# Reordering the entry of a blocked attention loop: the first score blocks ahead of most of the work on the character side

## What is computed

```python
# char = layernorm(x) [256, 512], ctx [25088, 512]
Q_char = char @ Wq_c.T + bq_c;  K_sub = ctx @ Wk_s.T + bk_s;  V_sub = ctx @ Wv_s.T + bv_s
char2sub = softmax(Q_char @ K_sub.T / sqrt(512)) @ V_sub
Q_sub = ctx @ Wq_s.T + bq_s;  K_char = char @ Wk_c.T + bk_c;  V_char = char @ Wv_c.T + bv_c
sub2char = softmax(Q_sub @ K_char.T / sqrt(512)) @ V_char      # 25088 rows
sub2char = interp_linear(sub2char, 256)                        # needs only 512 of those rows
gate = sigmoid(concat(char2sub, sub2char) @ Wg.T + bg)
x = x + gate * char2sub + (1 - gate) * sub2char
x = x + half_causal_attention(layernorm(x))                    # 16 heads of 64
x = x + mixture_of_experts(layernorm(x))                       # 32 routed experts and a shared one
```

## Time and profile before

| what | value |
|---|---|
| median of 3 runs | 1209.76 us (1207.69 to 1210.89) |
| span of the profiled execution, first to last instruction | 1206.7 us |
| TensorE matmul busy | 1061.1 us (88%) |
| TensorE weight load busy | 728.2 us (60%) |
| VectorE busy | 601.5 us (50%) |
| ScalarE busy | 387.8 us (32%) |
| chain that ended last, by engine | PE 71%, DMA 25%, DVE 2%, ACT 1% |
| moved by DMA | 381.44 MB, mean 316 GB/s |

### The profile page before, as it was taken

How to read it: one execution, slowest core, us unless ns; L and a number is a source line. 1 busy time by engine, 2 the same in 40 slices (tenths; PEclk the granted TensorE clock), 3 DMA queues, 4 the chain that set the end, 5 groups by cost and what they waited for, 6 DMA issues and landing times.

```text
span 1206.7 us, 16020 instructions
## 1 busy us (share of the span) xinstructions
PE 1061.1 (88%) x6374; PEld 728.2 (60%) x6374; DVE 601.5 (50%) x894; ACT 387.8 (32%) x594; POOL 3.5 (0%) x20
## 2 busy tenths in 40 slices
PE   8989999999999999999999999999876665656566
PEld 7767888878888888888766657664422222222223
DVE  2368878878878888788643365221211111111111
ACT  1245556556455465465422162100100000000000
POOL 1000000000000000000000000000000000000000
PEclk9999999999999999999999999999998989889899
DMA  9167899887787787788838305999999999999996
GB/s 351 62 209 281 311 344 333 302 311 270 270 309 272 269 309 270 272 293 278 282 129 356 134 7 228 428 426 425 363 426 426 430 429 427 426 430 427 428 427 275
DMA packets 89824, 381.44 MB, mean 316 GB/s; under 512 B 5569, under 2 KB 5697, under 8 KB 72769
## 3 DMA queue, kind: packets, MB, share of 16 engines
q1 hardware_dynamic: 89792, 381.00, 81.4%
HBM read 355.29 MB, written 25.69 MB: 316 GB/s over the span
## 4 chain that ended last, share of the span: by engine, by line
PE 71%; DMA 25%; DVE 2%; ACT 1%; issue 0%; SPq 0%; DVEq 0%
DMA wd<-in_r_down 24%; PE ps L579 7%; PE ps L578 7%; PE ps L577 7%; PE ps L591 7%; PE ps L592 7%; PE ps L590 7%; PE ps L957 3%; PE ps L880 3%; PE ps L550 2%; PE ps L563 2%; PE ps L932 2%; PE ps L967 2%; PE ps L938 2%; PE ps L901 1%; PE ps L914 1%
## 5 line engine op out<-in xcount | busy, mean ns | idle before, releaser
L577 PE MATMUL ps<-ctt_hi,q_hi 128*128 128x512 f32 x392 | 155.8, 397 | 4.4 <-ACT ctt_hi L1007 4.4
L579 PE MATMUL ps<-ctt_hi,q_lo 128*128 128x512 f32 x392 | 155.7, 397 | 0.0
L578 PE MATMUL ps<-ctt_lo,q_hi 128*128 128x512 f32 x392 | 155.7, 397 | 0.0
L591 PE MATMUL ps<-nat_lo,pt_hi 128*128 128x512 f32 x368 | 146.2, 397 | 0.0
L592 PE MATMUL ps<-nat_hi,pt_lo 128*128 128x512 f32 x368 | 145.0, 394 | 0.0
L590 PE MATMUL ps<-nat_hi,pt_hi 128*128 128x512 f32 x368 | 143.3, 389 | 0.4 <-DVE pt_lo L1251 0.3
L1559 DVE TENSOR_TENSOR hh<-sg,ps 128x256 f32<-128x256 f32 x32 | 13.5, 422 | 249.8 <-PE ps L938 249.8
L957 PE MATMUL ps<-wd,hh_t 128*32 128x512 f32 x512 | 78.9, 743 | 62.6 <-DMA wd<-in_r_down 57.4
L1011 ACT ACTIVATE nat_hi<-nat 128x2048 fp32r<-128x2048 f32 x48 | 92.0, 1917 | 82.9 <-DMA nat<-in_ctx_rows 82.9
L1241 DVE TENSOR_TENSOR ctt_lo<-ctt,ctt_hi 128x2048 fp32r<-128x2048 f32 x49 | 110.7, 2289 | 9.7 <-ACT ctt_hi L1007 9.7
L1246 DVE TENSOR_TENSOR nat_lo<-nat,nat_hi 128x2048 fp32r<-128x2048 f32 x48 | 109.9, 2289 | 6.1 <-ACT nat_hi L1011 4.3
(11 more groups left out here) (273 smaller groups left out, 1280.9 us busy)
## 6 DMA issues: line engine op xcount, KB each, us to landing
wu<-in_r_up SPq DMA_DIRECT2D x32, 2048.0 KB, 41.1
wd<-in_r_down SPq DMA_DIRECT2D x32, 2048.0 KB, 40.3
wg<-in_r_gate SPq DMA_DIRECT2D x31, 2048.0 KB, 39.2
ctt<-in_ctx_t SPq DMA_DIRECT2D x49, 1024.0 KB, 7.9
nat<-in_ctx_rows SPq DMA_DIRECT2D x48, 1024.0 KB, 7.3
strips<-turned SPq DMA_DIRECT2D x96, 256.0 KB, 5.5
pt<-strips SPq DMA_DIRECT2D x24, 1024.0 KB, 4.8
w_gate<-in_w_g_t SPq DMA_DIRECT2D x2, 1024.0 KB, 12.4
```

The source lines that it names most:

```text
L577: mm(o, qh, ctt_hi[par][:, c, :], start=(c == 0), stop=False)
L578: mm(o, qh, ctt_lo[par][:, c, :], start=False, stop=False)
L579: last = mm(o, ql, ctt_hi[par][:, c, :], start=False, stop=(c == HC - 1))
L591: mm(o, p_hi[:, w, :], n_lo[:, t, :], start=False, stop=False)
```

## The change

Nothing is computed differently; instructions and transfers change places, and buffers move so that they may.

- TensorE: `cb` goes to bank 5 and `bias2` to bank 4; then come `scores(0)`, the `w_qs` product (now in banks 6 and 7), `scores(1)`, the `sel_t` product, `vc`, `scores(2)`, the transposes of `pavg` with 12 dummy matmuls instead of 14, `s2c`, `scores(3)`, the transposes of `s2c`, and the products of the first pair.
- ScalarE: `ctt_hi` of blocks 0 and 1 moves ahead of `kc_t`; the splits of `nat` and `ctt`, the exps of the first pair and `pt_hi` of the first pair move ahead of the copies for `pavg_t` and `s2c`.
- VectorE: `q_lo` no longer waits for `cb`; the first pair's maxima, bias and turns move ahead of the work on `sc2`; the second pair is written out.
- SP: `ctt` of blocks 0 and 1 is loaded right behind `w_qs`, `nat` of blocks 0 and 1 next, and `w_vc`, `rows` and `w_gate2` behind them. The load of `nat[1]` waits for nothing any more.
- SBUF: `c_t`, `bias2` and `bqs_rep` lie where `s2c` and `s2c_t` will be; `sc2`, `pavg`, `pavg_t`, `kq_t` and `vc` where `w_qc` and `w_ks` were; `xn` where `pt` will be.

```diff
@@ buffers @@
-        xn = at("xn", [P, QT, D], F32, o)
-        c_t = at("c_t", [P, HC, NQ], F32, o + 4096)
+        xn = at("xn", [P, QT, D], F32, RINGB + 10 * kb)
+        c_t = at("c_t", [P, HC, NQ], F32, shared_low + 20480)
+        bias2 = at("bias2", [P, NQ], F32, shared_low + 24576)
+        bqs_rep = at("bqs_rep", [P, HC, P], F32, shared_low + 25600)
...
+        o = RINGB + 12 * kb
+        sc2 = at("sc2", [P, 4, NQ], F32, o)
+        pavg = at("pavg", [P, QT, NQ], F32, o + 4096)
+        pavg_t = at("pavg_t", [P, QT, NQ], F32, o + 6144)
+        o = RINGB + 13 * kb
         kq_t = at("kq_t", [P, HC, NQ], F32, o)
         vc = at("vc", [P, QT, D], F32, o + 4096)
@@ SP @@
-            sp.dma_start(rows[:, :], a["bias_rows"].partition_broadcast(P)).then_inc(s["rows_loaded"], 16)
...
-            sp.dma_start(flat(w_vc), runs(a["w_vc_t"])).then_inc(s["wvc_loaded"], 16)
-            sp.dma_start(sel_t[:, :, :], chunks(a["sel_t"])).then_inc(s["sel_loaded"], 16)
             load_columns(0, 0)
             load_columns(1, 1)
+            sp.dma_start(sel_t[:, :, :], chunks(a["sel_t"])).then_inc(s["sel_loaded"], 16)
+            load_rows(0, nat[0], nat_loaded[0])
+            load_rows(1, nat[1], nat_loaded[1])
+            sp.dma_start(flat(w_vc), runs(a["w_vc_t"])).then_inc(s["wvc_loaded"], 16)
+            sp.dma_start(rows[:, :], a["bias_rows"].partition_broadcast(P)).then_inc(s["rows_loaded"], 16)
             sp.dma_start(w_gate2[:, :, :], chunks(a["w_g_t"][D:2 * D, :])).then_inc(s["wg2_loaded"], 16)
-            load_rows(0, nat[0], nat_loaded[0])
...
             spread(0)
-            sp.wait_ge(s["s2c_in_psum"], 1)
-            load_rows(1, nat[1], nat_loaded[1])
@@ TensorE @@
-            pe.wait_ge(s["kc_ready"], 1)
-            pe.wait_ge(s["wqs_loaded"], 16)
-            weight_stationary(by_chunk(2), w_qs, kc_t, HC, s["kq_in_psum"])
             pe.wait_ge(s["rep_ready"], 1)
             for c in range(HC):
-                last = mm(ps[:, 1, 0:NQ], bqs_rep[:, c, :], kc_t[:, c, :], start=(c == 0), stop=(c == HC - 1))
+                last = mm(ps[:, 4, 0:NQ], bqs_rep[:, c, :], kc_t[:, c, :], start=(c == 0), stop=(c == HC - 1))
...
+            pe.wait_ge(s["qlo_ready"], 1)
+            scores(0, 0, banks_taken=False)
+
+            pe.wait_ge(s["wqs_loaded"], 16)
+            weight_stationary(by_chunk(6), w_qs, kc_t, HC, s["kq_in_psum"])
+
+            scores(1, 1, banks_taken=False)
...
-            keep_warm(14, 5)
+            keep_warm(12, 5)
```

More of the change, by code:

```diff
@@ L657, in _ @@
             last.then_inc(s["sc2_in_psum"], 1)
-            scores(0, 0, banks_taken=False)
-            scores(1, 1, banks_taken=False)
+            pe.wait_ge(s["bias2_ready"], 1)
+            pe.wait_ge(s["cb_ready"], 1)
+            pe.wait_ge(s["wvc_loaded"], 16)
+            for t in range(QT):
+                for c in range(HC):
+                    last = mm(ps[:, 4 + t, :], c_t[:, c, t * P:(t + 1) * P], w_vc[:, c, :], start=(c == 0), stop=(c == HC - 1))
+            last.then_inc(s["vc_in_psum"], 1)
+            scores(2, 0)
+            pe.wait_ge(s["vc_ready"], 1)
             pe.wait_ge(s["pavg_ready"], 1)
-            pe.wait_ge(s["vc_ready"], 1)
             transposes(pavg, ps[:, 4, :].rearrange("p (c n) -> p c n", n=NQ), s["pavgt_in_psum"], QT, QT)
-            keep_warm(14, 5)
+            keep_warm(12, 5)
             pe.wait_ge(s["pavgt_ready"], 1)
@@ L1026, in exps, with pair @@
                 act.activation(alpha[par], dmax, ACT.Exp).then_inc(s["alpha_ready"], 1)
[L1028 removed]
+            def pair(u, par):
                 columns_hi(u * 2 + 1, 1, u * 16 + 16)
[L1031 to L1033 removed]
                 rows_hi(u - 1, 0)
                 probs_hi(u - 1, 0)
[L1036 to L1037 removed]
+                act.wait_ge(s["products_done"], u * 2 - 2)
                 probs_hi(u - 1, 1)
@@ L1067, in _ @@
             last.then_inc(s["p2_ready"], 1)
+            for half in range(2):
+                probs_hi(0, half)
             act.wait_ge(s["pavgt_in_psum"], 1)
             act.activation(pavg_t[:, :, :], ps[:, 4, :].rearrange("p (c n) -> p c n", n=NQ), ACT.Copy).then_inc(s["pavgt_ready"], 1)
-            exps(0, 0)
-            columns_hi(2, 0, 32)
-            pair(1, 1, first=True)
+            act.wait_ge(s["s2c_in_psum"], 1)
+            act.activation(s2c[:, :, :], bank(6, 2), ACT.Copy).then_inc(s["s2c_ready"], 1)
+            columns_hi(4, 0, 48)
+            exps(1, 1)
             with act.Fori(1, NS // 2 - 1) as i:
@@ L1330, in _ @@
                                      ALU.mult, ALU.subtract).then_inc(s["qlo_ready"], 1)
+            dve.wait_ge(s["cb_in_psum"], 1)
+            dve.tensor_scalar(cb, ps[:, 5, 0:2], XSCALE, None, ALU.mult).then_inc(s["cb_ready"], 1)
+            dve.wait_ge(s["cb_ready"], 1)
             dve.wait_ge(s["bias2_in_psum"], 1)
-            dve.tensor_copy(bias2[:, :], ps[:, 1, 0:NQ]).then_inc(s["bias2_ready"], 1)
-            dve.wait_ge(s["rows_loaded"], 16)
-            dve.wait_ge(s["vc_in_psum"], 1)
-            for t in range(QT):
-                last = dve.tensor_tensor(vc[:, t, :], ps[:, 4 + t, :], r_vc, ALU.add)
-            last.then_inc(s["vc_ready"], 1)
-            columns_lo(0, 0)
-            columns_lo(1, 1)
+            dve.tensor_copy(bias2[:, :], ps[:, 4, 0:NQ]).then_inc(s["bias2_ready"], 1)
+            rows_lo(0, nat[0], nat_hi[0], nat_lo[0])
+            block_max(0, 0)
+            columns_lo(2, 0)
+            rows_lo(1, nat[1], nat_hi[1], nat_lo[1])
+            step(block_max(1, 1))
+            pair_bias(0)
+            for half in range(2):
+                turn(half, half)
+            columns_lo(3, 1)
             dve.wait_ge(s["sc2_in_psum"], 1)
@@ L1348, in _ @@
             dve.tensor_scalar(neg2, max2, -XSCALE, None, ALU.mult).then_inc(s["neg2_ready"], 1)
+            dve.wait_ge(s["rows_loaded"], 16)
+            dve.wait_ge(s["vc_in_psum"], 1)
+            for t in range(QT):
+                last = dve.tensor_tensor(vc[:, t, :], ps[:, 4 + t, :], r_vc, ALU.add)
+            last.then_inc(s["vc_ready"], 1)
             dve.wait_ge(s["p2_ready"], 1)
```

69 lines of the change are left out of this document (28 added, 41 removed).

## The result

| | before | changed |
|---|---|---|
| median of 10 runs each, us | 1209.41 (1207.69 to 1213.03) | **1202.74** (1200.14 to 1206.67) |
| ratio, 95% interval | | **0.995 (0.9939 to 0.9962)** |
| span of the profiled execution, us | 1206.7 | 1199.6 |

The change makes the kernel 0.5% faster: 6.7 us between the medians, 4.6 to 7.4 us by the interval, 7.1 us between the two profiled spans. Forecast were 1203.0, a gain of 6.7 and a span of 1200.0.

What follows compares the result with a forecast made beforehand. TensorE bounds the kernel, its entry pause being one of order on ScalarE. Pause 4.4, clock 1.5, late products 0.5, dummies 0.1, rounding 0.2 make 6.7 us: 1209.76 - 6.7 = 1203.1, stated as 1203.0; range 1201.0 to 1207.5.

Steps and rivals of the forecast that it cites:

- The pause and its clock: TensorE's entry at `scores(2)`: the wait for `ctt_hi` of block 2 costs 4.4 us, the lowered clock behind it 1.5 us.
- The sum: TensorE's entry rows laid end to end in the new order: loop's first matmul at 94.5 against 101.25, 6.7 us less.
- `ctt` ahead of `kc_t`: ScalarE's entry: two copies of 1.92 us go first; `kc_t` ends near 26.6, `cb` starts at 31.14; cost nothing.
- Block 2: Entry: its columns, issued at 40.5, are transferred and split by 50; `scores(2)` starts at 66.5, 16 us to spare.
- The first pair's chain: Entry, from the second block's maximum to `pt_hi`: moves 13.5 us ahead as one chain; `pt_hi` runs 70.4 to 72.4.
- The tight place: `pavg_t` behind `pt_hi` on ScalarE: free at 72.4, needed at 72.8; priced at nothing below, 1.5 us above.
- All of it carries to the end: Behind the entry: the experts' DMA stream starts earlier by as much as TensorE, so all 6.7 us reach the span.
- The products that follow get `pt` no later than they do now. Nothing.: Second pair, for the products after the first pair's: `pt` comes no later than before; cost nothing.
- A: Rival: small new waits in the entry, 1 to 3 us, giving 1204 to 1206, or 1207.5 with dropped clock; chance 0.14.
- B: Rival: entry transfers of `ctt` blocks 0 and 1 land at 31 instead of 23.1, giving 1207.9; chance 0.05.
- C: Rival: the gain is lost behind the loop and the time stays at 1209.8; chance 0.07.
- D: Rival: slower, as `pt_hi` ahead of `pavg_t` ties TensorE to the DRAM trip; 1214.1 at 10 us late; chance 0.04.

Runs made afterwards that it cites:

- the six above: Six profiles keeping the change's order in the loop, or moving only the weight loads in it; waits for `pt_lo` there sum to 0.8 to 3.5 us.
- the single edit: The kernel before with only block 2's split moved (`ctt_hi` ahead of `pavg_t`, `ctt_lo` behind the first pair's bias): 1210.57 us, ratio 1.0003.
- `pavg_t` first: The changed kernel with `pavg_t` ahead of `pt_hi` on ScalarE again, as it was before: 1202.36 us.
- the late entry: The changed kernel with 60 more dummy matmuls (3.6 us) between `bias2` and `scores(0)`: 1205.84 us, ratio to before 0.9953.
- both edits: The changed kernel with strips of pairs 1 and later stored before the `nat[0]` load, and attention weights loaded two pairs later: 1277.24 us.
- strips first: The changed kernel with SP storing the strips of pairs 1 and later before it loads `nat[0]`: 1277.92 us, ratio to before 1.054.

## Why the prediction was right, point by point

**The pause and its clock** (4.4 and 1.5 us). Right. The pause is gone from the rows and `scores(2)` runs at the full clock. Filling the pause with dummies took back 1.55 us of the entry alone.

**The sum** of 6.7 us. The entry lost 6.62. The loop's first matmul was put at 94.5, and it came at 93.70, where the earlier `w_qc`, which no step of mine covers, gave 0.9 us.

**The number as a whole.** That the median fell within 0.3 us of the forecast is in part luck. The loop gave back 2.0 us in this profile, and 0.8 to 3.5 in the six above, which I had put at nothing. Against it stood 1.7 us behind the loop, which I had not forecast either: in the profile of before the clock fell at 690.7, and of the nine profiles whose loop is not slowed throughout, the four in which it fell in the attention (before, the filled pause, the single edit, `pavg_t` first) need 614.2 to 614.6 us from the last block's first scores to the end, the five others 612.5 to 613.5. Whether the change makes this fall rarer, the record doesn't show.

**`ctt` ahead of `kc_t`** (landing by 23.1, slack 4.5 us). The second block landed at 22.1. With the old order of transfers it landed at 31.2, and 3.8 us of the entry went; so moving the two loads was needed for the gain.

**Block 2** (both parts done by 50, needed at 66.5). Its copy ran at 44.71 on ScalarE, behind `q_hi` and the first `nat_hi`, and `scores(2)` began at 65.19 without a pause.

**The first pair's chain** (`pt_hi` at 70.4). It came at 69.20, or 70.1 with the early start taken out. **`pavg`** was put at 70.1 with 2 us to spare; its last operation ended at 69.57, or 70.5 on the same footing, and TensorE's transposes began at 71.20, 1.6 us later.

**The tight place** (slack 0.4 us, priced at zero). Right: `pt_hi` was done 0.6 us before `pavg_t` could start, undoing the order changed nothing, and making the trip 1.9 us later on GpSimd cost 1.2. The 6.15 us that the prediction set beside its 4.8 are, in the Trainium skill's page "DMA: Bandwidth & Descriptors", section "Bandwidth", the figure for a 1 MB transfer issued from GpSimd. SP issues `pt`, and it took 4.79 us; the one that GpSimd issued with nothing beside it took 5.7.

**All of it carries to the end.** Right, by the profiles: with the entry 3.4 us longer the stage behind the loop kept its 612.5 us, and the timing alone could not have told. The engines had as much to do as before (TensorE's matmuls were busy 1061.1 and 1061.2 us), and the time fell all the same.

**"The products that follow get `pt` no later than they do now. Nothing."** This step was wrong. Pair 1 and pair 2 waited 0.56 and 1.46 us for `pt_lo` in the first profile, 0.95 and nothing in the second. I had moved the first pair's trip as a chain of rows, but for the second pair I looked at TensorE's and VectorE's dates only, and not at what stood ahead of its strips in SP's queue. SP's issues of the kernel before show the load and the strips of pair 1:

```profile
95.90 0.37 SPq L333 DMA_DIRECT2D nat<-in_ctx_rows  x1
97.56 3.82 SPq L341 DMA_DIRECT2D strips<-turned  x4
```

There VectorE had the turns ready 1.7 us after the load was issued. In the changed kernel they were ready before it, so the strips went out 0.4 us behind a 1 MB load and took 6.4 to 7.7 us to land instead of 4.5 to 5.7. Counted from the first products, the strips went out 1.2 us earlier than before (6.3 instead of 7.5 us) and the last of them landed 0.75 us later (15.9 instead of 15.2). In the profile of before `pt_lo` was just in time for pair 1, so this became the wait of 0.56 us. The reading fits the rows, but it is argued: the run that was to test it also moved the load.

**The rivals.** A did not come true in the entry, which has no new wait; waits of its size came in the loop, from one pair later on. B was kept away by the order of the loads. C is refuted by the profile with the late entry. D needs a trip that is 5.6 us late; the latest one seen, on GpSimd, was 1.9 us late.

## What to carry to other kernels

A pause has a queue of successors: before one moves the late step alone, one should ask which wait ends last once it is gone. Here the single edit gained nothing, and the whole reordering, which moves the next chain along, gained 6.7 us. Rows laid end to end in the new order predicted TensorE's part of the entry to a tenth of a microsecond (6.7 against 6.62), and the same has to be done for the transfer queue, pair by pair, until the loop is in its steady state. In the profiles of before and of the change `pt_lo` is ready at most one microsecond before TensorE needs it (but for the last pair), and a plausible reordering of the transfers cost ten times what the change gained. And a shift of 3 us is at the limit of what medians from different chips can tell: a stage's length, read from two profiles, told it at once.

## What was not expected of the hardware

- **Half the clock can follow a wait of under 2 us, and the wait's length alone does not decide.** In the second profile of the change TensorE waited 1.88 us for `w_qc`, here by its timeline:

```profile
10.04 0.76 PE L547 MATMUL ps<-c_t,w_qc 128*128 128x128 f32 x2 [1.88 <-DMA w_qc<-in_w_qc_t]
```

  The window behind it has a granted clock of 0.50, so 1.2 GHz:

```profile
10.00:13.00 3.00, 2.96 (x14) 2.99 (x15) 0.00 (x0) 0.00 (x0) 0.00 (x0) 0.50 1.00 368
```

  At this place the profiles with waits of 1.6 (the old order of transfers), 1.9 (both edits, GpSimd's queue and this one) and 2.2 us (strips first) have 3.4 us at 0.50, beginning between 0.7 us ahead of the wait's end and 0.4 us behind it. Those with 0.2, 0.5 (the change), 0.9, 1.1, 1.5 (before), 1.7 and 1.7 us have none. So the clock fell once with 1.6 us, and twice it did not with 1.7. The wait and the clock together move the first `w_kc` matmul between 15.9 and 19.4 us over the twelve profiles, which is more than half of the scatter of the timed runs (5.3 and 6.5 us for before and the change). A fall came behind the 1.93 us at `cb` above too, 2 us after that wait's end.

  A place in the attention shows it with equal waits, in the kernel before and then in the changed one:

```profile
690.49 0.41 PE L797 MATMUL ps<-k_t,q_t 64*128 64x128 f32 x2 [1.90 <-ACT patt L1130]
```

```profile
685.05 0.38 PE L798 MATMUL ps<-k_t,q_t 64*128 64x128 f32 x2 [1.90 <-ACT patt L1134]
```

  In the first the clock falls to 0.50 at 690.7, in the second it stays at 1.00. All twelve profiles have this wait of 1.9 us. In six of them the clock falls here, at this wait or at the one of 1.4 us behind it; in the other six it does not.
- **The same two transfers cost more through GpSimd's queue.** `pt` of 1 MB took 7.0 us instead of 4.8 over the whole loop, though GpSimd had nothing else to do and issued it in 0.6 us. The first one, with nothing beside it, took 5.7.
- **The place of one load in SP's written order decided some 71 us.** In the changed kernel TensorE waits only 2.0 us in the whole loop for what the two transfers bring; with the load behind the strips it waits 46.7.
